# Who waits for a finished cell: ScalarE instead of GpSimd

## Chip, cores and metric

One NeuronCore of a Trainium2 chip runs the whole program. The time is that of the device for one execution, in microseconds (us); given is the median of several executions.

## What is computed

A graph block on 6250 nodes of 256 features and 200000 edges. With `xn` the normalised rows, three parts are added to `x`: a graph network of two layers, an attention without softmax, and after a second normalisation a router with two of eight experts.

```python
def _gnn_layer(x, row, col, W, b, g, beta):
    neigh = x[col]
    agg = jax.ops.segment_sum(neigh, row, num_segments=n)
    deg = jax.ops.segment_sum(jnp.ones((row.shape[0],), x.dtype), row, num_segments=n)
    deg = jnp.maximum(deg, 1.0)[:, None]
    h = (x + agg / deg) @ W.T + b
    ...
    return jax.nn.silu(hn)

x = x + _L0_gnn_ref(xn, edge_index, ...) + _L0_mix_ref(xn[None], ...)[0]
x = x + _L0_ffn_ref(_layernorm(x, axis=-1)[None], ...)[0]
```

The sum over neighbours is computed as a product with a dense matrix: `counts[source row, target column]` is how many edges lead from one node to the other. The change lies where this matrix is made.

## The kernel before

**The stages.** (1) To about 570 us: the edges' keys are sorted on VectorE with turns on TensorE, beside the attention's products. (2) From 571 to 1470 us: the count matrix is made, cell by cell. (3) To about 2000 us: the first graph layer, for which TensorE multiplies slabs of the count matrix with the table of rows (lines 1252, 1253). (4) The second layer (line 1255), and (5) from about 2600 us the experts.

**The count matrix.** It is cut in G = 637 cells: 13 row groups of 512 rows (`rg`), the last with 128 rows only, times 49 column blocks of 128. The sorted edges are cut in chunks of 128. A step is one chunk against one cell; there are STEPS = 2200 of them in a fixed walk through chunks and cells, and which step is the last of a cell depends on the edges. For a step, VectorE makes two one-hot tiles of the chunk's edges, 128 x 128 for the columns (`hot_c`, line 1946, eight steps at a time) and 128 x 512 for the rows (`hot_r`, line 1951), and TensorE multiplies them into the cell's bank of PSUM (line 1218). The steps are taken in groups of four; VectorE may be twelve `hot_r` tiles ahead.

**The banks.** Four banks take the cells in turn. When a cell's last step is done, ScalarE copies the bank, times 0.25, to `held` (line 866, semaphore `s_cell`) and clears it (line 867, `s_free`). After seven cells (`CW`) it stores them to the array `counts` in memory (line 870); the store waits for its last copy (`s_cell`), and the copy that reuses the half of `held` waits for the store of fourteen cells before (`s_held`, line 861). SyncE is the gate: for each group of four steps it loads from `cell1` which cell the group's last step belongs to, waits until `s_free` says that this cell's bank is clear, and increments `s_gate` (line 585); TensorE waits for `s_gate` and for VectorE's tiles (`s_hot`) before each group.

**Who knows that a cell is done.** TensorE increments `s_step` at each step. `ends` holds for each cell the number of steps after which it is complete; it is in SBUF, and becomes known only when the program runs. GpSimd walks through the cells: it loads `ends[g]` in a register (line 105, the helper `loaded`), waits until `s_step` has that value and increments `s_done` (line 696). ScalarE waits for `s_done >= g + 1`.

**What else is on GpSimd.** At cell 200 (`REST_AT`) it waits for the heavy cells (`s_heavy`) and writes their remainders to `rest` (line 693). Behind the loop it gathers the heavy rows of the table (`heavy_rows(0)`, line 706), when the table of 25 pairs has been written (line 542, `s_tab`), and then adds a bias to the rows of the first four pairs (`bias`, line 709), when `s_lo[0]` says that the table's low parts are made. Each further addition waits for a pair of the first layer. VectorE waits for the bias (`s_bias`) when it makes a pair's sums (`z_tile`, line 1983 and on).

Beside the steps run, in groups of fixed number, the output product of the attention (lines 1177, 1179), the table (lines 1910, 1911), the next pieces of the walk (lines 1083 to 1087, 1703), and from group 416 on the first 25-column halves of the first layer's sums (lines 1197, 1198).

Of the kernel before, what the change touches and what calls it, by code (L numbers as in the profile page):

```python
# [45 lines left out]
G = NRG * NCB  # L46
# [18 lines left out]
STEPS = -(-(NCH + G - 1) // 4) * 4  # L65
# [38 lines left out]
def loaded(nc, ap, engine, most):  # L104
    return nc.values_load_multi_w_load_instructions(
        ap, engines=(engine,), min_val=1, max_val=most,
        skip_runtime_bounds_check_because="one plus a cell's number, or a count of steps: both from the staircase")[1]
# [33 lines left out]
SLAB_AT = {**{AHEAD_AT - 4 + k: k for k in range(4)}, **{AHEAD_LAST[k] + 2: 4 + k for k in range(4)}}  # L141
assert len(SLAB_AT) == 8 and max(SLAB_AT) < STEPS // 4

REST_AT = 200

XF_BANKS = (0, 1, 3)
XF_LOWS = ((0, 2), (2, 3), (3, 5), (5, 7), (7, 9))
# [49 lines left out]
def gps_layer(nc, x, src, dst, w0, b0, g0, be0, w1, b1, g1, be1, wq, wkv, wo, bo,  # L197
              wr, br, fw1, fb1, fw2, fb2, ga, be, out):
    ctx = ExitStack()
    with ctx:  # L200
        def sb(name, shape, dt=F32):
            return ctx.enter_context(nc.sbuf_tensor(name, shape, dt))

        def sem(name):
            return ctx.enter_context(nc.semaphore(name))
# [9 lines left out]
        rest = nc.dram_tensor("remainders", [RB << 2 * CB_SH, 1], F16, kind="Internal").ap()  # L215
# [29 lines left out]
        hval = sb("heavy_value", [P, 2], F16)  # L245
# [40 lines left out]
        ends = outer[0:1, 10176:10496].bitcast(U16)  # L286
# [20 lines left out]
        h_cell, h_node, h_tmp, h_part = (heavy[:, n:n + 1].bitcast(I32) for n in (1, 2, 3, 4))  # L307
# [94 lines left out]
        s_heavy, s_hcell = sem("heavy_cells"), sem("heavy_cells_written")  # L402
# [3 lines left out]
        s_upto, s_uptop, s_ends = sem("cells_reached"), sem("cell_ends_product"), sem("cell_ends")  # L406
        s_hot, s_step, s_free = sem("one_hots"), sem("steps_done"), sem("cell_banks_free")

        s_gate, s_done = sem("groups_open"), sem("cells_done")
        s_cell, s_held = sem("cells_copied"), [sem("cells_stored0"), sem("cells_stored1")]  # L410
        s_xin, s_spill = [sem("x_pair_in0"), sem("x_pair_in1")], [sem("residual_out0"), sem("residual_out1")]
        s_dve = sem("dve_chain")
# [66 lines left out]
        def _(sp):  # L479
# [149 lines left out]
            with sp.Fori(1, NP - 1) as p:  # L629
                load_slabs(1, p)  # L630
            load_slabs(1, NP - 1, 1)

            sp.wait_ge(s_pick, 1)
            _, chosen = nc.values_load_multi_w_load_instructions(small[0:1, 64:66].bitcast(I32), engines=(mybir.EngineType.SP,),
                                                                 min_val=0, max_val=NE - 1)
            for k, v in enumerate(chosen):
# [18 lines left out]
        def _(pool):  # L655
# [30 lines left out]


            pool.wait_ge(s_zeroed, 16)
            pool.wait_ge(s_ends, 1)
            for g in range(G):  # L690
                if g == REST_AT:
                    pool.wait_ge(s_heavy, 1)
                    pool.indirect_dma_start(rest, bass.IndirectOffsetOnAxis(ap=h_cell, axis=0), hval[:, 0:1], None).then_inc(s_hcell, 16)
                end, = loaded(nc, ends[:, g:g + 1], mybir.EngineType.Pool, STEPS)
                pool.wait_ge(s_step, end)
                pool.sem_inc(s_done, 1)  # L696

            def affine(l, p):
                pool.wait_ge(s_nr[l], p + 1)
# [53 lines left out]
        def _(act):  # L753
# [100 lines left out]
            act.activation(hkeys, sort[home[ROUNDS]], ACT.Copy).then_inc(s_conv, 1)  # L854


            for g in range(G):
                b, c = g // CW % 2, g % CW
                act.wait_ge(s_done, g + 1)
                if c == 0 and g >= 2 * CW:  # L860
                    act.wait_ge(s_held[b], g // (2 * CW) * 16)
                rg, cb = g // NCB, g % NCB - c

                q = min(GR // P, RB - rg * (GR // P))
                cell_bank = bank[(g + 1) % NBK][:, 0:q * P]
                act.activation(held[:, b, 0:q, c, :], cell_bank.rearrange("p (q r) -> p q r", r=P), ACT.Copy, scale=0.25).then_inc(s_cell, 1)  # L866
                act.activation(cell_bank, cell_bank, ACT.Copy, scale=0.0).then_inc(s_free, 1)  # L867
                if c == CW - 1:
                    act.wait_ge(s_cell, g + 1)
                    act.dma_start(slabs[rg * GR:rg * GR + q * P, cb * P:(cb + CW) * P].rearrange("(q p) c -> p q c", p=P),  # L870
                                  held[:, b, 0:q, :, :].rearrange("p q c r -> p q (c r)")).then_inc(s_held[b], 16)
# [1418 lines left out]
```

## Time and profile before

| | us |
|---|---|
| median of 3 executions | 2919.98 (2918.04 to 2920.64) |
| the profiled execution | 2923.55 |
| its span, first to last instruction | 2921.8 |
| busy TensorE / VectorE / ScalarE / GpSimd | 2512.2 / 1878.7 / 1402.6 / 199.0 |

The profile is of one execution with the hardware profiler. PE is TensorE's matmul, PEld its weight load, DVE VectorE, ACT ScalarE, POOL GpSimd, SP SyncE; a q behind the name is the engine's queue, whose own work (register loads, waits, issues of DMAs) is not counted as busy. "L866 ... <- POOLq L696" is a wait of line 866 that GpSimd's line 696 ended. Instructions of an engine overlap at their ends, so the distance from start to start is shorter than the duration.

### The profile page before, as it was taken

The numbers are of one execution on the slowest core, as the hardware profiler recorded it, in microseconds if no ns is written. First come the engines' busy times: TensorE is split into PE (matmuls) and PEld (weight loads), VectorE is DVE, ScalarE is ACT, GpSimd is POOL, SyncE is SP. The second block draws the span as 40 slices with busy tenths as digits, with TensorE's granted clock in tenths as the row PEclk, the third lists the DMA queues.
The fourth block names the chain that finished last, engine by engine and source line by source line (L and its number), as shares of the span: only waits on it lengthen the run. The fifth ranks groups of instructions, "written<-read, shape, count | busy, mean of one in ns | idle before, by whom it ended". The sixth has DMA issues, their size and how long they took to land. (4 is left out here: it accounts for less than half of the span.)

```text
span 2921.8 us, 50327 instructions
## 1 busy us (share of the span) xinstructions
PE 2512.2 (86%) x14013; PEld 1458.1 (50%) x14013; DVE 1878.7 (64%) x4792; ACT 1402.6 (48%) x3753; POOL 199.0 (7%) x185
## 2 busy tenths in 40 slices
PE   0877677685889888889999999997999999969997
PEld 0444444332334343334378888883444444445665
DVE  8898887899999999999953222221333333366555
ACT  0877566265777667687821211211222222246665
POOL 0000000000000000000011111100111111115000
PEclk9998899698999999999999999998999999979999
DMA  5000000022245344243275555556444444410000
GB/s 182 19 15 15 11 15 15 17 76 76 89 146 185 116 162 161 103 165 136 102 256 185 157 162 165 157 162 208 140 135 140 141 135 141 140 33 15 22 22 31
DMA packets 167927, 318.02 MB, mean 109 GB/s; under 512 B 30227, under 2 KB 139540, under 8 KB 167764
## 3 DMA queue, kind: packets, MB, share of 16 engines
q1 hardware_dynamic: 115860, 230.55, 24.7%
q10 hardware_dynamic: 51776, 85.24, 8.0%
q8 instruction: 78, 1.28, 0.2%
q14 instruction: 85, 0.70, 0.1%
q0 software_dynamic: 128, 0.26, 0.1%
HBM read 203.09 MB, written 112.92 MB: 108 GB/s over the span
## 5 line engine op out<-in xcount | busy, mean ns | idle before, releaser
L1255 PE MATMUL banks<-outer,ring 128*128 128x512 f16 x2450 | 540.0, 380 | 18.6 <-DMA outer<-table,heavy 11.6
L866 ACT ACTIVATE ring<-banks 128x512 f16<-128x512 f32 (+1 forms) x637 | 365.6, 574 | 291.0 <-POOLq L696 287.9
L1252 PE MATMUL banks<-tabs,ring 128*128 128x257 f16 x2250 | 495.0, 274 | 3.3 <-DMA ring<-counts 3.3
L1253 PE MATMUL banks<-tabs,ring 128*128 128x256 f16 x2250 | 494.9, 273 | 0.0
L1255 PEld LDWEIGHTS banks<-outer,ring 128*128 128x128 f16 x2450 | 240.2, 98 | 299.8 <-issue 23.1
L867 ACT ACTIVATE banks<-banks 128x512 f32<-128x512 f32 (+1 forms) x637 | 367.0, 576 | 0.0
L1951 DVE TENSOR_SCALAR ring<-val,outer 128x512 f16<-128x512 f16 x1102 | 315.1, 345 | 20.0 <-PE banks L1218 19.9
L1218 PE MATMUL banks<-ring 128*128 128x512 f16 x920 | 261.4, 393 | 41.4 <-DVE ring L1951 20.1
L893 ACT ACT_TABLE_LOAD x50 | 64.2, 1283 | 377.7 <-DVE row_stats L2005 377.7
L1252 PEld LDWEIGHTS banks<-tabs,ring 128*128 128x128 f16 x2250 | 220.6, 98 | 31.8 <-issue 4.0
L1253 PEld LDWEIGHTS banks<-tabs,ring 128*128 128x128 f16 x2250 | 220.5, 98 | 25.8
L1024 PE MATMUL banks<-tabs,xT 128*128 128x512 f32 x400 | 203.3, 634 | 0.0
L1983 DVE TENSOR_SCALAR uinv<-banks 128x1 f32 (+1 forms) x49 | 7.7, 158 | 296.0 <-PE banks L1253 280.9
L1218 PEld LDWEIGHTS banks<-ring 128*128 128x128 f16 x920 | 85.6, 98 | 188.7 <-issue 133.9
L1951 DVE TENSOR_SCALAR outer<-val,outer 128x512 f16<-128x512 f16 x549 | 169.3, 345 | 7.5 <-PE banks L1218 7.1
L1408 PE MATMUL banks<-big,ring 128*128 128x256 f16 x1176 | 147.2, 275 | 20.8 <-DVE ring L2240 20.7
L1951 DVE TENSOR_SCALAR big<-val,outer 128x512 f16<-128x512 f16 x549 | 159.3, 345 | 0.0
L1395 PE MATMUL banks<-outer,big 128*128 (+2 forms) x624 | 147.8, 373 | 4.2 <-DVE big L2184 4.2
L2240 DVE SCALAR_TENSOR_TENSOR ring<-ring,product_scales 128x512 f16<-128x512 f32 (+1 forms) x104 | 83.0, 808 | 100.7 <-ACT ring L980 100.5
L1218 PE MATMUL banks<-outer,ring 128*128 128x512 f16 x276 | 94.0, 390 | 60.4 <-DVE big L1951 45.3
L1408 PEld LDWEIGHTS banks<-big,ring 128*128 128x128 f16 x1176 | 113.7, 98 | 59.9 <-DVE ring L2240 27.7
L2002 DVE BATCH_NORM_STATS2 row_stats<-xn 128x6 f32 (+1 forms) x100 | 37.4, 416 | 152.2 <-ACT xn L887 152.2
(391 smaller groups left out, 3816.7 us busy)
## 6 DMA issues: line engine op xcount, KB each, us to landing
counts<-ring ACTq DMA_DIRECT2D x84, 896.0 KB, 4.1
ring<-counts SPq DMA_DIRECT2D x94, 800.0 KB, 4.7
ring<-counts SPq DMA_DIRECT2D x94, 768.0 KB, 4.1
outer<-in_fw SPq DMA_DIRECT2D x8, 1024.0 KB, 8.2
outer<-in_x SPq DMA_DIRECT2D x5, 1280.0 KB, 13.5
x_transposed<-xT SPq DMA_DIRECT2D x50, 128.0 KB, 1.7
outer<-in_x SPq DMA_DIRECT2D x25, 256.0 KB, 3.0
xT<-x_transposed SPq DMA_DIRECT2D x25, 256.0 KB, 2.8
```

The costliest lines, as they stand in the source:

```text
L866: act.activation(held[:, b, 0:q, c, :], cell_bank.rearrange("p (q r) -> p q r", r=P), ACT.Copy, scale=0.25).then_inc(s_cell, 1)
L867: act.activation(cell_bank, cell_bank, ACT.Copy, scale=0.0).then_inc(s_free, 1)
L893: act.activation(std_of(n, b), var_of(n, b), ACT.Sqrt, bias=eps_c[:, :]).then_inc(s_std[n], 1)
L1024: m = mm(bank[4 + h], xT[t % 2][:, c * P:(c + 1) * P], wkv_s[:, c * 1024 + h * 512:c * 1024 + (h + 1) * 512], start=c == 0, stop=c == DC - 1)
L1218: mm(ps[:, bass.ds(at, 512)], hot_c[t // 8 % 3][:, t % 8, :], hot_r[t % RSLOTS], start=False, stop=False, skip_group_check=True).then_inc( ...
L1252: mm(o[:, 0:D + 1], a, xtab[l][:, COLUMN[cb], D:2 * D + 1], start=cb == 0, stop=False)
L1253: m = mm(o[:, 0:D], a, xtab[l][:, COLUMN[cb], 0:D], start=False, stop=cb == NT - 1)
L1255: m = mm(o, a, xtab[l][:, COLUMN[cb], 0:2 * D], start=cb == 0, stop=cb == NT - 1)
L1395: m = mm(bank[4 + j % 4][:, 0:nt * P], w1p[:, a, w:w + P], xfp[:, bass.ds(g * 4, nt), b * D + c * P:b * D + (c + 1) * P], start=c == a == ...
L1408: m = mm(bank[q][:, 0:D], hp[:, j % 4, a, q * P:(q + 1) * P], w2p[:, b, j * D:(j + 1) * D], start=j == a == b == 0, stop=j == FJ - 1 and a ...
L1951: ins = dve.tensor_scalar(hot_r[t % RSLOTS], iota16[:, 0:GR], row_v[:, q % 2, u:u + 1], None, op0=ALU.is_equal)
L2240: dve.scalar_tensor_tensor(hp[:, j % 4, 1, 0:w], hid[j % 2][:, 0:w], fsc[:, 2:3], hp[:, j % 4, 0, 0:w], op0=ALU.mult, op1=ALU.subtract).th ...
```

## The change

ScalarE loads `ends[g]` in a register of its own, once for each cell, and waits for `s_step` itself. GpSimd's loop of 637 loads, waits and increments, and the semaphore `s_done`, are gone. The write of the remainders no longer stands at cell 200 of that loop but alone, behind its wait for the heavy cells; what stood behind the loop on GpSimd follows it directly.

```diff
--- before.py
+++ after.py
@@ -141,7 +141,6 @@
 SLAB_AT = {**{AHEAD_AT - 4 + k: k for k in range(4)}, **{AHEAD_LAST[k] + 2: 4 + k for k in range(4)}}
 assert len(SLAB_AT) == 8 and max(SLAB_AT) < STEPS // 4
 
-REST_AT = 200
 
 XF_BANKS = (0, 1, 3)
 XF_LOWS = ((0, 2), (2, 3), (3, 5), (5, 7), (7, 9))
@@ -406,7 +405,7 @@
         s_upto, s_uptop, s_ends = sem("cells_reached"), sem("cell_ends_product"), sem("cell_ends")
         s_hot, s_step, s_free = sem("one_hots"), sem("steps_done"), sem("cell_banks_free")
 
-        s_gate, s_done = sem("groups_open"), sem("cells_done")
+        s_gate = sem("groups_open")
         s_cell, s_held = sem("cells_copied"), [sem("cells_stored0"), sem("cells_stored1")]
         s_xin, s_spill = [sem("x_pair_in0"), sem("x_pair_in1")], [sem("residual_out0"), sem("residual_out1")]
         s_dve = sem("dve_chain")
@@ -686,14 +685,8 @@
 
 
             pool.wait_ge(s_zeroed, 16)
-            pool.wait_ge(s_ends, 1)
-            for g in range(G):
-                if g == REST_AT:
-                    pool.wait_ge(s_heavy, 1)
-                    pool.indirect_dma_start(rest, bass.IndirectOffsetOnAxis(ap=h_cell, axis=0), hval[:, 0:1], None).then_inc(s_hcell, 16)
-                end, = loaded(nc, ends[:, g:g + 1], mybir.EngineType.Pool, STEPS)
-                pool.wait_ge(s_step, end)
-                pool.sem_inc(s_done, 1)
+            pool.wait_ge(s_heavy, 1)
+            pool.indirect_dma_start(rest, bass.IndirectOffsetOnAxis(ap=h_cell, axis=0), hval[:, 0:1], None).then_inc(s_hcell, 16)
 
             def affine(l, p):
                 pool.wait_ge(s_nr[l], p + 1)
@@ -854,9 +847,11 @@
             act.activation(hkeys, sort[home[ROUNDS]], ACT.Copy).then_inc(s_conv, 1)
 
 
+            act.wait_ge(s_ends, 1)
             for g in range(G):
                 b, c = g // CW % 2, g % CW
-                act.wait_ge(s_done, g + 1)
+                end, = loaded(nc, ends[:, g:g + 1], mybir.EngineType.Activation, STEPS)
+                act.wait_ge(s_step, end)
                 if c == 0 and g >= 2 * CW:
                     act.wait_ge(s_held[b], g // (2 * CW) * 16)
                 rg, cb = g // NCB, g % NCB - c
```

ScalarE's instructions around a store, before. `cells_done` is `s_done`, `cells_copied` is `s_cell`, `cells_stored0` is one of `s_held`:

```order
L866 ACTIVATE ring<-banks 128x4x128 [waits cells_done]
L867 ACTIVATE banks<-banks 128x512
L870 DMA counts<-ring 128x4x896 [waits cells_copied]
L866 ACTIVATE ring<-banks 128x4x128 [waits cells_stored0,cells_done]
L867 ACTIVATE banks<-banks 128x512
```

The same place with the change (its lines 861, 862 and 865 are 866, 867 and 870 of before); `steps_done` is `s_step`:

```order
L861 ACTIVATE ring<-banks 128x4x128 [waits steps_done]
L862 ACTIVATE banks<-banks 128x512
L865 DMA counts<-ring 128x4x896 [waits cells_copied]
L105 TENSOR_LOAD outer
L861 ACTIVATE ring<-banks 128x4x128 [waits cells_stored0,steps_done]
L862 ACTIVATE banks<-banks 128x512
L105 TENSOR_LOAD outer
```

A load stands in front of each copy, and behind the store's issue where there is one; the copy waits for the steps where it waited for GpSimd.

GpSimd between the last fill of stage 1 and the first loop of the first layer, before:

```order
L685 MEMSET tabs 128x2048 [waits dots_added]
L105 TENSOR_LOAD outer [waits cell_ends,remainders_cleared]
L105 TENSOR_LOAD outer [waits steps_done] x199
L693 DMA remainders<-heavy_value,heavy 802816x1 [waits steps_done,heavy_cells]
L105 TENSOR_LOAD outer
L105 TENSOR_LOAD outer [waits steps_done] x436
L706 DMA tabs<-table,heavy 128x512 [waits steps_done,table0_written]
L709 TENSOR_TENSOR xn<-xn,big 128x512 [waits table0_low]
L709 TENSOR_TENSOR xn<-xn,big 128x512 x3
```

and with the change (its lines 689, 699 and 702 are 693, 706 and 709 of before):

```order
L684 MEMSET tabs 128x2048 [waits dots_added]
L689 DMA remainders<-heavy_value,heavy 802816x1 [waits heavy_cells,remainders_cleared]
L699 DMA tabs<-table,heavy 128x512 [waits table0_written]
L702 TENSOR_TENSOR xn<-xn,big 128x512 [waits table0_low]
L702 TENSOR_TENSOR xn<-xn,big 128x512 x3
```

None of the three waits for `steps_done` any more, only for its own data.

## Rows read from the trace of the kernel before

**Rows 1.** Busy us (instructions) by stretch: PE, PEld, DVE, ACT, POOL; clock, DMA, GB/s
```profile
606.00:1441.00 835.00, 712.78 (x2982) 294.75 (x2979) 812.03 (x2560) 599.39 (x1158) 1.19 (x1) 0.96 0.37 130
1441.00:1470.00 29.00, 22.66 (x107) 9.29 (x107) 25.34 (x81) 19.45 (x92) 0.00 (x0) 1.00 0.18 69
```

**Rows 2.** Groups by line, 571 to 1471 us: busy us, mean ns, idle before
```profile
L1951 DVE TENSOR_SCALAR ring<-val,outer 128x512 f16<-128x512 f16 x1101 | 314.8, 345 | 20.0 <-PE banks L1218 19.9
```

**Rows 3.** Waits, 606 to 1441 us: us in total, times, longest
```profile
ACT ring L866 <- POOLq L696: 237.0, 186, 23.2
...
PE banks L1218 <- SPq L585: 32.2, 49, 1.7
...
DVE ring L1951 <- PE banks L1218: 16.4, 25, 3.5
```

**Rows 4.** The same, 1441 to 1470 us
```profile
PE banks L1218 <- SPq L585: 6.8, 14, 0.8
DVE ring L1951 <- PE banks L1218: 2.5, 5, 0.7
```

**Rows 5.** Instructions of lines 105 and 870: duration in ns, min/median/max
```profile
L105 POOLq TENSOR_LOAD <-outer x637: 268/274/1333, 570.1 to 1469.4; - x160
L870 ACTq DMA_DIRECT2D counts<-ring x91: 338/378/451, 592.7 to 1470.1; - x91
```

**Rows 6.** Order of time from 1280 us: start and duration in us
```profile
1280.27 0.70 PE L1218 MATMUL banks<-outer,ring 128*128 128x512 f16 x2
...
1281.06 0.60 ACT L866 ACTIVATE ring<-banks 128x512 f16<-128x512 f32 x1 [0.23 <-POOLq L696]
```

**Rows 7.** Order of time from 300 us
```profile
300.71 1.91 PE L1031 MATMUL banks<-big,xT 128*128 128x256 f32 x4
...
302.66 0.38 ACT L768 ACTIVATE xn<-banks 128x256 f32<-128x256 f32 x1 [1.41 <-PE banks L1031]
```

**Rows 8.** Order of time on ScalarE from 1301 us
```profile
1302.47 0.61 ACT L866 ACTIVATE ring<-banks 128x512 f16<-128x512 f32 x1
...
1303.46 0.61 ACT L866 ACTIVATE ring<-banks 128x512 f16<-128x512 f32 x1
1303.94 0.62 ACT L867 ACTIVATE banks<-banks 128x512 f32<-128x512 f32 x1
1304.11 0.38 ACTq L870 DMA_DIRECT2D counts<-ring  x1
1304.76 0.60 ACT L866 ACTIVATE ring<-banks 128x512 f16<-128x512 f32 x1 [0.20 <-POOLq L696]
```

**Rows 9.** ScalarE at 2094 us: order of time, and line 878 alone
```profile
2094.00 1.28 ACT L893 ACT_TABLE_LOAD   x1 [2.30 <-DVE row_stats L2005]
L878 ACTq ALU_OP  x1: 35/35/35, 2094.1 to 2094.1; - x1
```

**Rows 10.** Lines 542 and 709, and busy time in two stretches
```profile
L542 SPq DMA_DIRECT2D table<-tabs x25: 359/367/463, 830.9 to 1267.8; - x25
L709 POOL TENSOR_TENSOR xn<-xn,big x25: 1252/1265/1276, 1471.6 to 1917.3; 128x512 f32 x21, 128x512 f32<-128x512 f32 x4
1270.00:1277.00 7.00, 5.60 (x21) 1.91 (x20) 7.00 (x25) 5.15 (x11) 0.00 (x0) 1.00 0.70 234
1281.00:1441.00 160.00, 150.42 (x779) 67.58 (x779) 159.44 (x532) 138.48 (x272) 0.00 (x0) 1.00 0.39 139
```

**Rows 11.** Line 2240 in two stretches of equal length, and line 749
```profile
2635.00:2671.00 36.00, 19.84 (x14) 1.00 0.00 1
2671.00:2707.00 36.00, 9.56 (x13) 1.00 0.09 30
L749 POOL TENSOR_TENSOR xn<-xn,xT x25: 1258/1710/1722, 2635.1 to 2670.4; 128x512 f32 x25
```

**Rows 12.** Order of time at 1477 us, and a wait from 1466 to 1500
```profile
1477.59 0.38 PE L1252 MATMUL banks<-tabs,ring 128*128 128x257 f16 x1 [2.70 <-DMA ring<-counts]
DVE uinv L1983 <- PE banks L1315: 15.1, 1, 15.1
```

## The prediction

> **What bounds the kernel now.** I read the views in this order: busy time by stretch, groups by line, waits, and then the order of time at single places. The change touches one stretch, from 571 to 1470 us, in which 637 cells of the count matrix are made. In its body, 606 to 1441 us, VectorE is busy for 812.0 of 835 us, 97%, TensorE for 712.8 and ScalarE for 599.4 [rows 1]. VectorE's share is the one-hot tiles of line 1951 [rows 2]: it is the pacer, and a microsecond taken from ScalarE is worth nothing there by itself. The last 49 cells are another matter: from 1441 to 1470 us VectorE is busy 25.3 of 29 us, TensorE 22.7, ScalarE 19.5, so no engine is full and the loop from step to copy to gate sets the pace [rows 1].
>
> The waits say how much hangs on the part that changes. In the body ScalarE sits idle for 237.0 us in front of line 866 until GpSimd signals a cell, but that is mostly ScalarE having nothing to do: the signal comes when the step has been done. What counts is who waits for ScalarE: TensorE waits for SyncE's gate 49 times, 32.2 us together, and VectorE, the pacer, waits for TensorE in front of the largest group of line 1951 for 16.4 us [rows 3]. In the last 29 us TensorE waits for the gate 14 times, 6.8 us together, about half a microsecond in each group of four steps, and VectorE 2.5 us [rows 4]. That is the room that a faster signal could win.
>
> **The signal.** Removed are 637 loads, 637 waits and 637 increments on GpSimd. Their time there was free; what they cost is the hop. At 1280.97 us (1280.27 + 0.70) the matmul that ends a cell is over, and ScalarE starts at 1281.06: 0.09 us [rows 6]. Where ScalarE waits for TensorE itself, the matmul of 302.62 us (300.71 + 1.91) is followed at 302.66: 0.04 us [rows 7]. So 0.05 us is saved for each cell for which ScalarE stands waiting. Of these, only a signal in front of a gate that TensorE stands at, and whose delay VectorE then feels, shortens the run: the 14 gates of the end [rows 4], and I take about 7 of the 49 in the body, since VectorE is full through most of them. 21 x 0.05 = 1.0 us gained. The bound below is that every gate counts, 63 x 0.05 = 3.2 us.
>
> **The load on ScalarE.** Added are 637 loads in ScalarE's queue. On GpSimd one takes 0.274 us, the longest 1.33 [rows 5]. ScalarE works off cells that are ready at one per 0.99 us (1302.47 to 1303.46) [rows 8]. Is the load beside that or added to it? Two rows say beside. The store of line 870 is issued at 1304.11 while the clearing of line 867 runs until 1304.56 [rows 8]. And at 2094.1 the queue does a register operation of line 878, which stands behind an activation, while the table load in front of that activation has just begun, at 2094.00, and has 1.28 us to go [rows 9]. So the queue runs ahead of the engine; 0.27 us hides under the copy and the clearing of the cell before, and even a load of 0.9 us would. I cost it at nothing inside a block of seven. If the cover goes, the price is in the first rival.
>
> The exception is the seventh cell. Its store waits in the queue for the copy, takes 0.38 us to issue [rows 5], and only behind it can the next load start. The issue ended at 1304.49 [rows 8], and the load adds its 0.27 us and the steps around it, together some 0.32 us, to the earliest start of the next copy. There are 90 such places. Most have slack, as here, where the next cell was ready only at 1304.76. I take it that six are in front of a gate that matters, four of the seven in the last stretch, where cells come at the pace of the loop, and two in the body: 6 x 0.32 = 1.9 us lost. The bounds are 0 and, if 30 places counted, 9.6 us. The Trainium skill gives a `tensor_load` a floor of about 600 ns (DMA: Bandwidth & Descriptors, Latency and other measured facts); by it the six places would cost 2 us more, as an estimate; the trace has 0.274 us, and the sum goes by that.
>
> **What GpSimd does with its freedom.** Behind its loop stand three things that now come early. The write of the remainders moves from behind cell 200 to the moment the heavy cells are known; nobody waits for it until the slabs are read. The gather of the heavy rows moves from behind the last cell to shortly after the last write of the table, issued at 1267.8 [rows 10]. And the first four bias additions of line 709, 1.265 us each, follow it [rows 10]. Before, they began at 1471.6 us, while VectorE waited 15.1 us for TensorE [rows 10, 12]. Now they fall in about 1270 to 1277 us, where it is busy for 7.00 of 7.00 us [rows 10]. What they would do beside line 1951 no row shows. The nearest rows: from 2635 to 2671 us GpSimd adds (line 749) while VectorE runs line 2240, 14 instructions in 19.84 us, 1.42 each; in the next 36 us, without GpSimd, 13 take 9.56, 0.74 each; and GpSimd's own addition is stretched from 1.26 to 1.71 us [rows 11]. In the 1.71 us of one addition VectorE thus does 1.71 x 0.74 / 1.42 = 0.89 us of work and loses 0.82. Four additions: 3.3 us. The end below is 0 (line 1951 has one tile input, where 2240 has two), a gain is excluded, since nothing that VectorE waits for in the stage comes from GpSimd; the end above is the whole of the additions, 4 x 1.265 = 5.1 us. I take 3.3, from the only contended pair of the trace. VectorE is full for 159.4 of the 160 us behind it, so it is carried to the end of the stretch [rows 10].
>
> Having these early buys nothing: the next stretch begins with TensorE waiting for slabs, until 1477.59 us, and the first use of sums by VectorE waits for TensorE's line 1315, not for the bias [rows 12]. The stretch behind is bound by TensorE and is only shifted.
>
> **The sum.** -1.0 + 1.9 + 3.3 = +4.2 us. The profiled execution took 2923.55 us (span 2921.8), 3.6 above the median of the runs, 2919.98. The terms are differences, so I put them on the median: 2924.2, rounded to 2924.0.
>
> **Rivals.**
> - *The load does not hide* (7%). If the queue takes the load only when the clearing has ended, a ready cell costs 0.48 to the clearing, 0.62 for it, 0.27 for the load: at least 1.37 us instead of 0.99. 588 large cells x 1.37 = 806 us, the 49 small ones some 35, and 84 stores x 0.38 = 32: 873 of 899 us, and since cells come in bursts it would be the bound for much of the time; I price it at +40 us, 2960. It decides from the point where ScalarE's time per cell passes 1.4 us, the stretch's 899 / 637. Against it stand [rows 8, 9].
> - *GpSimd takes VectorE's inputs for the whole of each addition* (18%): VectorE stands still for 5.1 us, and ten store places count instead of six: -1.0 + 3.2 + 5.1 = +7.3, 2927.3. For it: 1951 is full just there [rows 10]. Against: in [rows 11] both engines slow down, neither stops. The Trainium skill says this outright: the loser of the shared port "fully blocks" (SBUF — State Buffer, Who interferes with whom); these rows don't bear the word "fully" out.
> - *The additions cost nothing* (25%), because VectorE's tiles come first and GpSimd works in between: +0.9, or with three store places 0: 2920 to 2921. For it: one tile input.
> - *The hop counts more* (12%). The long loads, up to 1.33 us [rows 5], now and then made GpSimd late; a queue that runs ahead takes them out. If each of the 63 gates gives 0.05 (3.2 us), the late signals at the end another 4, and the additions cost nothing, the time is 2913.
>
> The rest, 38%, is my forecast.
>
> **How the numbers follow.** 0.2% of the time, 5.8 us, is about what a measurement of this kernel can tell from no change. The forecast (+4.2) and the third rival (+0 to +1) lie within it, with a part of the forecast's own spread beyond: same 0.55. Slower: rivals one and two, 0.25, and 0.07 of the forecast: 0.32. Faster: most of the last rival, and a little of the third: 0.13. The range leaves out the first rival and the outer half of the last one: 2914 to 2931, the upper end being full blocking (+5.1) with some 20 store places (+6.4) less the hop.
>
> **What would show it.** Right: in the changed profile line 105 stands in ScalarE's queue 637 times at about 0.27 us; copies in a burst still start 0.99 us apart; a copy starts 0.04 us behind its matmul; behind a store the next copy starts 0.3 us later than before; the additions of the bias stand near 1272 us with VectorE's instructions beside them at over 0.35 us, and the last cell is copied at about 1474 us, not just before 1470. Wrong: a pitch of 1.3 us or more (the first rival), tiles of line 1951 that keep their 0.345 us through the additions [rows 2] (the third), or a stretch between 1441 and 1470 us that is shortened by more than 1 us (the last).

## The result, and the profile after

The changed kernel takes 2926.78 us in the median of 15 executions (2920.74 to 2930.55), the kernel before 2918.67 us (2915.99 to 2923.71) beside it on the same chip. The two medians lie 8.1 us apart. The ratio estimated from all executions is 1.0023, with a 95% interval of 1.0015 to 1.0031: slower by 0.23%, some 4 to 9 us, 6.7 by its middle. The range, 2914 to 2931, holds the time. The predicted 2924.0 is 2.8 too low, but that flatters it: the kernel before was 1.3 us faster here than in the three executions that the forecast started from. As a difference, +4.2 was forecast and +6.7 to +8.1 measured.

The spans of the two profiled executions, 2921.8 and 2923.7 us, show 1.9 us of that, because the first stage happened to end 5 us earlier in the later one. So all comparisons of traces below start at the first step and count from there. The largest group of the steps' matmuls in the changed kernel, which holds the first and the last of the 2200 (how many, duration in ns, start of the first and of the last):

```profile
L1213 PE MATMUL banks<-ring x920: 379/380/634, 566.9 to 1472.1; 128*128 128x512 f16 x184
```

Before, the same row says 572.0 to 1469.3. The 2200 steps thus take 905.2 us instead of 897.3: **7.9 us longer**.

(Lines shift a little: 1951, 866 and 870 of before are 1946, 861 and 865 in the changed kernel; in the experiments 1951 is 1946 to 1951.)

Busy time by stretch, as in [rows 1], the second stretch up to 1473 us since the last cell is later:

```profile
606.00:1441.00 835.00, 707.34 (x2954) 292.58 (x2952) 811.29 (x2543) 593.13 (x1146) 8.87 (x6) 0.96 0.37 128
1441.00:1473.00 32.00, 23.80 (x113) 9.65 (x113) 26.98 (x85) 20.53 (x99) 0.00 (x0) 1.00 0.20 72
```

VectorE is still the pacer, 811.3 of 835 us. TensorE has 5.4 us less to its name than before: fewer steps were done in the same time. Waits in the body, and from 1441 us on, to compare with [rows 3, 4]:

```profile
ACT ring L861 <- PE banks L1213: 238.7, 194, 23.1
...
PE banks L1213 <- SPq L584: 29.4, 46, 2.1
...
DVE ring L1946 <- PE banks L1213: 13.8, 25, 1.3
```

```profile
PE banks L1213 <- SPq L584: 8.0, 13, 1.1
DVE ring L1946 <- PE banks L1213: 3.7, 7, 0.8
```

ScalarE now waits for TensorE itself, 238.7 us against 237.0 for GpSimd's signal. TensorE's wait for the gate is 29.4 us instead of 32.2, and VectorE's for TensorE 13.8 instead of 16.4. In the tail it goes the other way: 8.0 us for the gate instead of 6.8, and 3.7 instead of 2.5. Neither is 7.9 us. Most of it stands in one place, in the order of time on VectorE (start, duration; a row holds up to six neighbours of a kind):

```profile
1265.65 0.68 DVE L1941 TENSOR_TENSOR ring<-outer 128x1024 f16<-128x1024 f16 x1
1266.26 0.34 DVE L1946 TENSOR_SCALAR outer<-val,outer 128x512 f16<-128x512 f16 x1
1266.52 6.03 DVE L1946 TENSOR_SCALAR big<-val,outer 128x512 f16<-128x512 f16 x3
1272.47 0.87 DVE L1946 TENSOR_SCALAR ring<-val,outer 128x512 f16<-128x512 f16 x3
```

The third row is three tiles that take 6.03 us; three of them take 0.87 elsewhere. The second of the three, from 1266.78 us, alone has 5.50 us. Beside it, GpSimd:

```profile
1264.48 2.71 POOL L699 DMA_INDIRECT tabs<-table,heavy  x1 [581.95 <-DMA table<-tabs]
1267.21 4.91 POOL L702 TENSOR_TENSOR xn<-xn,big 128x512 f32<-128x512 f32 x4
```

And busy time of each engine just before, in and behind the stretch (columns as in [rows 1]):

```profile
1260.00:1267.20 7.20, 5.06 (x19) 1.72 (x18) 7.20 (x23) 5.08 (x10) 2.71 (x1) 1.00 0.20 73
1267.20:1272.20 5.00, 0.09 (x1) 0.00 (x0) 5.00 (x1) 1.09 (x2) 4.91 (x4) 0.89 1.04 317
1272.20:1277.00 4.80, 4.12 (x10) 1.52 (x11) 4.80 (x17) 2.00 (x4) 0.00 (x0) 0.50 0.49 182
```

The four additions, 4.91 us, and VectorE's stop lie on one another. VectorE counts as busy for 5.00 of 5.00 us but finishes nothing; TensorE does 0.09 us of work, and as it starts again its granted clock is 0.50, the lower level of 1.2 GHz, in the stretch behind. The gather of line 699 takes 2.71 us here.

Step by step, the 7.9 us come together like this: 0.55 less up to step 1600, 5.46 more between steps 1600 and 1700, 1.5 more between 1800 and 1900, 0.2 more from there to 2130, and 1.35 more in the tail. The 1.5 goes with a drop of TensorE's granted clock to 0.50 at 1335.9 us. Such a drop is in eight of the twelve profiled executions of this document, and not in those of the kernel before and of experiments 2, 6 and 9. Whether the change makes it more frequent, no run shows.

ScalarE around a store, to be held against [rows 8]:

```profile
1302.24 0.61 ACT L861 ACTIVATE ring<-banks 128x512 f16<-128x512 f32 x1
...
1303.23 0.62 ACT L861 ACTIVATE ring<-banks 128x512 f16<-128x512 f32 x1
...
1303.88 0.38 ACTq L865 DMA_DIRECT2D counts<-ring  x1
1304.66 0.60 ACT L861 ACTIVATE ring<-banks 128x512 f16<-128x512 f32 x1 [0.32 <-PE banks L1213]
```

Copies that are ready start 0.99 us apart (1302.24 to 1303.23), as before. Behind the store the next copy starts 0.40 us after the issue has ended (1303.88 + 0.38 to 1304.66). That is its floor now: in 44 of the 90 places the distance is 0.39 to 0.41 us, and nowhere less. Before, it was 0.10 us in 35 of them, as here in the tail (1443.39 + 0.35 to 1443.84):

```profile
1443.39 0.35 ACTq L870 DMA_DIRECT2D counts<-ring  x1
1443.84 0.28 ACT L866 ACTIVATE ring<-banks 128x128 f16<-128x128 f32 x1 [0.31 <-issue]
```

And the loads themselves:

```profile
L105 ACTq TENSOR_LOAD <-outer x637: 257/263/1349, 565.0 to 1472.1; - x160
```

### The profile page after: what moved, and what is told of

It is laid out like the page before. It is cut to its first block and busy times, and to the rows that moved or that the text cites. A ratio compares the mean times of both kernels' runs of the same rounds, so it can differ in the third digit from the quotient of the medians.

```text
span 2923.7 us, 49690 instructions
## 1 busy us (share of the span) xinstructions
PE 2507.3 (86%) x14013; PEld 1456.0 (50%) x14013; DVE 1882.3 (64%) x4792; ACT 1400.1 (48%) x3753; POOL 200.7 (7%) x185
## 5 line engine op out<-in xcount | busy, mean ns | idle before, releaser
L1019 PE MATMUL banks<-tabs,xT 128*128 128x512 f32 x400 | 196.5, 615 | 0.0
L1403 PEld LDWEIGHTS banks<-big,ring 128*128 128x128 f16 x1176 | 114.0, 98 | 61.1 <-DVE ring L2235 28.6
L694 POOL TENSOR_TENSOR xn<-xn,big 128x512 f32 (+1 forms) x49 | 62.0, 1266 | 1155.0 <-DVE xn L2009 1115.9
```

The source lines that it names most:

```text
L1019: m = mm(bank[4 + h], xT[t % 2][:, c * P:(c + 1) * P], wkv_s[:, c * 1024 + h * 512:c * 1024 + (h + 1) * 512], start=c == 0, stop=c == DC - 1)
L1403: m = mm(bank[q][:, 0:D], hp[:, j % 4, a, q * P:(q + 1) * P], w2p[:, b, j * D:(j + 1) * D], start=j == a == b == 0, stop=j == FJ - 1 and a ...
```

## The experiments

Kernels were run in three sets, the kernel before beside each: its median was 2919.61 us in the first set (27 executions), 2920.84 in the second (33) and 2920.74 in the third (15). "Steps" is the time from the first to the last of the 2200 steps in the profiled execution, less that of before, cut at step 2130, where the small cells begin. One such number can be off by 1.5 us: where the drop of TensorE's clock near 1335 us occurs, the steps begin 1.2 to 1.5 us later from there on, and before's profile doesn't have it. A ratio from 10 or 11 executions has an interval of 0.09% to either side, 2.6 us.

### 1. The additions put back behind the last cell (first set)

```diff
@@ on GpSimd, ahead of the gather
+            pool.wait_ge(s_step, STEPS)
             heavy_rows(0)
```

> The change, but GpSimd waits for all 2200 steps before it gathers the heavy rows and adds the bias, so that both stand where they stood before the change. Theory A (GpSimd's four additions stop VectorE altogether): the instruction of 5.5 us on line 1946 is gone and no tile takes over 0.4 us; 5.2 us of the 8.1 come back, the median is some 2.5 us above the kernel before. Rival B (the load behind each store is the main cost, and the additions only stand beside VectorE): at most 1 us comes back, the median stays some 7 us above before.

Measured: 2919.44 us (11 executions), ratio 1.0005 (0.9996 to 1.0014). The long tile is gone. Steps: -0.28 us up to 2130, +1.72 in the tail. So ScalarE's loads and waits by themselves cost 1.5 us by the ratio, within the noise, where 2.5 us were expected. The new place of what stands behind the loop costs the difference between 1.0023 and 1.0005, 5.3 us, which can be off by 3.5; the trace has 5.46 us for it. This experiment moves gather and additions together; the next one parts them.

### 2. The gather early, the additions late (first set)

```diff
@@ on GpSimd
             heavy_rows(0)
+            pool.wait_ge(s_step, STEPS)
             pool.wait_ge(s_lo[0], NP)
```

> The change, but GpSimd waits for all steps between the gather of the heavy rows and the bias additions: the gather is early, the additions late. Theory A: the gather costs VectorE nothing although it takes 2.7 us itself, so the time is that of e1_late within 1 us. Rival B (a gather beside VectorE takes its port as well): 1 to 2.7 us above e1_late, with a tile of line 1946 of over 1 us near 1265 us.

Measured: 2919.52 us, 1.0002 (0.9993 to 1.0011). GpSimd, and VectorE's tiles beside the gather:

```profile
1265.06 3.96 POOL L699 DMA_INDIRECT tabs<-table,heavy  x1 [581.37 <-DMA table<-tabs]
1465.97 4.94 POOL L702 TENSOR_TENSOR xn<-xn,big 128x512 f32<-128x512 f32 x4 [196.95 <-PE banks L1214]
```

```profile
1266.98 0.87 DVE L1947 TENSOR_SCALAR big<-val,outer 128x512 f16<-128x512 f16 x3
```

The gather takes 3.96 us instead of the 0.97 that it took alone behind the last cell, but three of VectorE's tiles beside it take their 0.87 us. It is GpSimd's work that takes longer here. Steps 1600 to 1660 take what they took before, within 0.03 us. The cost is the additions' alone.

### 3. Eight additions early instead of four (first set)

```diff
-            for p in range(4):
+            for p in range(8):
                 bias(p)
```

with the loop behind it shortened by four.

> The change, with eight bias additions ahead of the loop where there are four, so that eight of them run in a row near 1267 us. Theory A (VectorE stands still for as long as GpSimd adds): one tile of line 1946 of about 10.4 us, and the time 5 us above the change's 2926.8, some 13 us above before. Rival B (my estimate of 0.82 us lost per addition, the rest from elsewhere): 3.3 us above the change. Rival C (the four additions are not what costs): no difference.

Measured: 2930.48 us (5 executions), 1.0039 (1.0025 to 1.0053). VectorE and GpSimd:

```profile
1268.47 10.89 DVE L1946 TENSOR_SCALAR big<-val,outer 128x512 f16<-128x512 f16 x3
```

```profile
1269.16 9.79 POOL L702 TENSOR_TENSOR xn<-xn,big 128x512 f32<-128x512 f32 x8
```

9.79 us of additions, and one tile of 10.37 us in the group of three. Twice the additions, twice the stop. Four more cost 0.16% more, 4.7 us, for 4.9 us of work. The ratios alone are too coarse to tell that from rival B's 3.3 us, and the time is 11 us above before, not 13. The traces do tell: the steps lose 10.14 us here and 5.46 with four, 4.7 us for four more. The stop is the whole of each addition, not a share of it.

### 4. The load ahead of the store (first set)

Experiment 1, and the next cell's load is issued behind the clearing, so that the store comes after it:

```diff
+            end, = loaded(nc, ends[:, 0:1], mybir.EngineType.Activation, STEPS)
             for g in range(G):
-                end, = loaded(nc, ends[:, g:g + 1], mybir.EngineType.Activation, STEPS)
                 act.wait_ge(s_step, end)
...
                 act.activation(cell_bank, cell_bank, ACT.Copy, scale=0.0).then_inc(s_free, 1)
+                if g + 1 < G:
+                    end, = loaded(nc, ends[:, g + 1:g + 2], mybir.EngineType.Activation, STEPS)
                 if c == CW - 1:
```

> As e1_late, and ScalarE loads the next cell's last step behind the clearing of the cell before it, ahead of the store's issue, so that no load stands behind a store. Theory A (the load behind the store costs 0.32 us where a gate waits for it): the first copy behind a store starts 1.1 us after the last one ahead of it, as before the change, not 1.4; the end of the stage, 1441 to 1470 us, is 1.3 to 2 us shorter than in e1_late, and the median falls 2 to 3 us below e1_late, to 0 to 1 us below before. Rival B (loads are hidden behind stores too): the same time as e1_late.

Measured: 2919.05 us, 0.9998 (0.9989 to 1.0007). Around a store:

```profile
1306.10 0.38 ACTq L868 DMA_DIRECT2D counts<-ring  x1
1306.58 0.60 ACT L862 ACTIVATE ring<-banks 128x512 f16<-128x512 f32 x1
```

The next copy follows the end of the issue by 0.10 us (1306.10 + 0.38 to 1306.58), as in the tail before the change. Steps: +0.24 us up to 2130, -0.42 in the tail, where experiment 1 had +1.72 and the other kernels with the load behind the store +1.3 to +1.8. The load behind a store thus costs 1.8 to 2.1 us, all of it in the seven places of the tail: 7 x 0.29 = 2.0. The median can't show it: 0.9998 and 1.0005 are 2.0 us apart, with intervals that overlap. Up to step 1600, experiments 1 and 4 lie at -1.7 and -1.2: the stores of the body cost nothing that shows.

### 5. Two loads for each cell, the first try (second set)

```diff
+                loaded(nc, ends[:, g:g + 1], mybir.EngineType.Activation, STEPS)
                 end, = loaded(nc, ends[:, g:g + 1], mybir.EngineType.Activation, STEPS)
```

> As e1_late, but ScalarE loads each cell's last step twice. Theory A (a load hides under the copy and the clearing, and shows only behind a store and between the small cells of the end): cells that are ready still follow each other at 0.99 to 1.01 us in the body; the first copy behind a store starts another 0.3 us later; from step 2130 to step 2199 the steps take 2 to 5 us longer than in e1_late (the small cells' pitch of 0.4 us can't hold two loads); the median is 2 to 6 us above e1_late. Rival B (loads add to each cell): a pitch of 1.27 us for ready cells and a median over 20 us above e1_late. Rival C (nothing of the load shows anywhere): the same time.

Measured: 2919.91 us, 0.9996 (0.9987 to 1.0005). But the trace has only 637 loads in ScalarE's queue: the compiler left out the one that nothing used. It is experiment 1 once more, and says nothing on its question; experiment 9 asks it again. It has a use as a measure of the noise: what is the same program came out at 1.0005 in the first set and at 0.9996 here.

### 6. Fills in place of the additions (second set)

The gather early and the additions late, as in experiment 2; in the additions' early place GpSimd fills three tiles of the same size that nobody needs then, so this is work added to the program:

```diff
+            for free in (g_s, xT[0][:, :], xT[1][:, :]):
+                pool.memset(free, 0.0)
+            pool.wait_ge(s_step, STEPS)
```

> As e2_gather_early (gather early, bias late), and GpSimd fills three tiles of 128x512 that nobody needs any more where the change has its additions, near 1268 us; they only write. Theory A (any instruction of GpSimd on SBUF stops line 1951, a read or not): one tile of it lasts as long as the three fills together, some 1.5 us more, and the time is 1.5 us above e2_gather_early. Rival B (it is the reads of the additions that stop VectorE): all tiles at 0.35 us, no difference.

Measured: 2922.0 us (10 executions), 1.0004 (0.9995 to 1.0013). VectorE and GpSimd:

```profile
1264.44 2.81 DVE L1949 TENSOR_SCALAR big<-val,outer 128x512 f16<-128x512 f16 x3
```

```profile
1265.11 0.54 POOL L706 MEMSET big<- 128x512 f32 x1
1265.57 1.00 POOL L706 MEMSET xT<- 128x512 f32 x2
```

The three tiles of VectorE take 2.81 us instead of 0.87, with 1.54 us of fills beside them, and steps 1600 to 1660 take 1.9 us longer. One of the three tiles alone has 2.29 us. That is read from the trace; the median, 1.0004 against 1.0002 in experiment 2, is too coarse to show 1.5 us. A fill reads nothing from SBUF, and it stops VectorE too. So it is not GpSimd's reading that collides.

### 7. The four additions spaced out (second set)

One each behind steps 1680, 1760, 1840 and 1920:

```diff
             for p in range(4):
+                pool.wait_ge(s_step, 1680 + 80 * p)
                 bias(p)
```

> The change, but GpSimd's four additions stand singly, behind steps 1680, 1760, 1840 and 1920, not in a row. Theory A (VectorE is the pacer, each addition takes it for 1.25 us wherever it stands in the body): four tiles of line 1946 of some 1.5 us, and the same time as the change, 7 to 8 us above before. Rival B (a stop of 1.25 us is absorbed by the twelve tiles that VectorE is ahead, only one of 5 us in a row reaches TensorE, and it is the fall of TensorE's clock behind the long stop that costs): 3 us or less above before.

Measured: 2924.95 us, 1.0016 (1.0007 to 1.0025). Steps 1600 to 2000: +5.6 us, of which some 1.3 is the clock's drop near 1335 us, by the other traces that have it. The first of the four, on VectorE and on GpSimd:

```profile
1285.94 0.68 DVE L1942 TENSOR_TENSOR ring<-outer 128x1024 f16<-128x1024 f16 x1
1286.54 1.35 DVE L1947 TENSOR_SCALAR outer<-val,outer 128x512 f16<-128x512 f16 x1
```

```profile
1285.04 2.71 POOL L702 TENSOR_TENSOR xn<-xn,big 128x512 f32<-128x512 f32 x1 [12.41 <-PE banks L1214]
```

A tile of 1.35 us instead of 0.34, four times. Both sizes were missed: the run is 4.7 us above before by its ratio (2 to 7), not 7 to 8 and not 3 or less. For rival B's reason nothing speaks: single stops do reach the steps, each by about 1 us. Spacing gains at most a little. Four lone tiles lose 1.0 us each against 5.2 for the one of the change, and the ratios, 1.0016 and 1.0023, overlap.

GpSimd's row is 2.71 us long, though an addition takes 1.26: it stands from 1285.04, through VectorE's tiles of line 1947. If its last 1.26 us are the work, they begin at 1286.49, close to the end of line 1942 (1286.62), which compares two inputs. The same holds, to 0.01 us, for all four here and for three of the four in experiment 8; the last one there began between two tiles of line 1947. So while VectorE goes from one such tile to the next GpSimd is mostly shut out, it comes in at the end of the other kind, and then shuts VectorE out.

### 8. The four additions in the tail (second set)

As 7, behind steps 2144, 2152, 2160 and 2168.

> The change, but the four additions stand behind steps 2144, 2152, 2160 and 2168, in the stretch of the small cells, where VectorE is not the pacer. Theory A (a stop costs where VectorE is full, and is free where the gate sets the pace): long tiles are there, but the time is that of e1_late within 1.5 us. Rival B (a stop costs wherever it falls): 4 to 5 us above e1_late.

Measured: 2921.27 us, 0.9999 (0.999 to 1.0008). The first addition on GpSimd:

```profile
1443.14 1.65 POOL L702 TENSOR_TENSOR xn<-xn,big 128x512 f32<-128x512 f32 x1 [172.90 <-PE banks L1214]
```

There are again four tiles of about 1.35 us, between 1443.6 and 1455.2 us, so VectorE is stopped as in 7. Yet the tail is 1.3 us longer than before and experiment 1's is 1.7 longer, experiment 2's 1.3: the stop costs nothing. VectorE has slack in the tail, as [rows 1, 4] say, and none in the body. The price of a stop is set by where it falls.

### 9. Two loads for each cell, both used (third set)

Experiment 1, with a load of the cell before and a wait on it as well:

```diff
+                if g:
+                    prev, = loaded(nc, ends[:, g - 1:g], mybir.EngineType.Activation, STEPS)
                 end, = loaded(nc, ends[:, g:g + 1], mybir.EngineType.Activation, STEPS)
+                if g:
+                    act.wait_ge(s_step, prev)
                 act.wait_ge(s_step, end)
```

> As e1_late (additions behind the last cell), with a second load per cell in ScalarE's queue, of the previous cell's last step, which a second wait uses, so that it stays in the program: 1273 loads. Theory A (the queue works ahead beside copy and clearing; only behind a store is the load in the open): inside a block ready copies still start 0.99 to 1.01 us apart, behind a store the next copy starts another 0.25 to 0.35 us later (store end to copy about 0.7 instead of 0.39), and the run is 1 to 5 us longer than e1_late: 1.0015 of before, about 2923. Rival (a load takes its time from the engine): ready copies start at least 0.25 us further apart, 1.25 or more, and the run is over 10 us longer.

Measured: 2968.15 us (5 executions), 1.0157 (1.0143 to 1.017): 46 us slower. Both theories missed. Away from the stores, ready large cells keep their pitch of 0.99 us, as theory A says, but the time is far past its 1 to 5 us. ScalarE behind a store in the body, and the loads of that stretch:

```profile
1303.99 0.38 ACTq L870 DMA_DIRECT2D counts<-ring  x1
1305.94 0.60 ACT L866 ACTIVATE ring<-banks 128x512 f16<-128x512 f32 x1 [1.50 <-PE banks L1218]
...
1307.44 0.60 ACT L866 ACTIVATE ring<-banks 128x512 f16<-128x512 f32 x1 [0.41 <-issue]
```

```profile
L105 ACTq TENSOR_LOAD <-outer x6: 262/366/865, 1304.4 to 1307.8; - x6
```

Loads issued while the store's data moves (it lands 4.1 us after its issue, in the median) are slow: here there are two of 0.85 and 0.87 among the six. In experiment 1, 87 of its 637 loads take over 0.7 us, the longest 1.37, and all of them start 0.8 to 3.4 us behind a store's issue. It is not ScalarE's queue that makes them slow: GpSimd's loads of before show the same behind stores, with 0.8 us in the mean 1 to 2 us after the issue. One load of 0.8 us hides under a large cell of 0.99 us; a slow one and a second one do not. Here the next copy starts 1.57 us behind the end of the issue (1303.99 + 0.38 to 1305.94), and the one after it another 1.50 us later. This place is worse than most for the first copy: its floor is 0.77 to 0.79 us behind a store, where experiment 1 has 0.39, which is what theory A expected. What theory A lacked is the second copy: it follows the first within 1.02 us behind 42 of 84 stores of large cells in experiment 1, and behind 4 here, where most take 1.6 to 2.0 us. The waits in the body:

```profile
PE banks L1218 <- SPq L584: 65.6, 75, 2.7
...
DVE ring L1951 <- PE banks L1218: 33.5, 46, 2.3
```

TensorE's wait for the gate is 65.6 us against 28.6 in experiment 1, VectorE's for TensorE 33.5 against 15.2. In the tail, first this kernel, then experiment 1:

```profile
1496.85 0.28 ACT L866 ACTIVATE ring<-banks 128x128 f16<-128x128 f32 x1 [0.75 <-PE banks L1218]
...
1497.55 0.28 ACT L866 ACTIVATE ring<-banks 128x128 f16<-128x128 f32 x1 [0.25 <-PE banks L1218]
...
1498.25 0.28 ACT L866 ACTIVATE ring<-banks 128x128 f16<-128x128 f32 x1 [0.25 <-issue]
```

```profile
1454.79 0.28 ACT L862 ACTIVATE ring<-banks 128x128 f16<-128x128 f32 x1 [0.69 <-PE banks L1214]
...
1455.16 0.27 ACT L862 ACTIVATE ring<-banks 128x128 f16<-128x128 f32 x1
...
1455.51 0.28 ACT L862 ACTIVATE ring<-banks 128x128 f16<-128x128 f32 x1
```

A small cell needs 0.70 us instead of 0.35 to 0.37: there the queue, not the engine, sets the pitch, and the second load and wait add 0.33 to 0.35 to each cell. Steps: +32.7 us up to 2130, +12.8 behind it. The cover under which one load hides is thus about one load deep.

### 10. The load ahead of the store and the gather early (third set)

Experiments 4 and 2 together.

> The load placed ahead of the store (as e4_ahead) and the gather of the heavy rows early, the additions behind the last cell (as e2_gather_early). Theory A: no tile of line 1946 or 1949 over 1 us near 1267 us, the tail from step 2130 to 2199 no longer than before, the run 2918 to 2920, within 0.1% of before. Rival (the early gather costs something that single profiles hid): 2 us or more above e4_ahead.

Measured: 2916.06 us (11 executions), 0.9986 (0.9977 to 0.9995), below the 2918 to 2920 expected. It is the one version that comes out ahead of the kernel before, by 0.14%, less than the 0.2% that such a comparison can be trusted with, and so ahead of the change by 0.37%. Its steps are 0.2 us longer than before's in the profiles, so the trace doesn't show where the 4 us lie, and the interval meets that of experiment 4; 0.12% between the two is little more than the 0.09% between experiments 1 and 5, the same program. That it is no slower than before is shown; that the early gather adds to it isn't.

## Why the prediction was right or wrong

The sum said +4.2 us: the signal -1.0, the load behind the store +1.9, the additions +3.3.

**The signal** is as forecast where it can be read directly. Of the copies that wait for their cell's last step, 212 of 220 start 0.09 us behind the matmul before, and 211 of 221 start 0.04 us behind it in experiment 4, with the load ahead of the store. In the changed kernel 189 of 244 do; the rest come up to 0.4 us later, because the load is late. What the signal is worth in the body is less certain. Up to step 1600, where nothing else has changed, the steps come 0.55 us earlier in the changed kernel, and between 0.6 and 1.9 earlier in experiments 1 to 8 and 10. But experiments 1 and 5, the same program, stand at 1.7 and 0.6. In the small cells there is a gain that the step didn't have: with GpSimd's walk their usual pitch was 0.40 us, with ScalarE's own it is 0.35 to 0.37. With the load out of the way of the store the tail is 0.4 us shorter than before (experiment 4). The forecast had 0.7 for the tail.

**The load hidden inside a block** held: the pitch of ready cells is 0.99 us. The reason given, that "even a load of 0.9 us would" hide, was needed: over 80 loads take 0.7 us or more, a few up to 1.35. What it lacked is how thin this cover is. The first rival's +40 us is about what the second load costs (experiment 9, +46), though not by its mechanism: away from the stores the pitch of ready large cells didn't move; it is behind stores and in small cells that the queue falls behind.

**The load behind the store** held in sum, 1.9 against 1.8 to 2.1, not in its places. All seven of the tail count, not four, and none in the body that shows, not two. The price of one was forecast at 0.32 and is 0.29 us. That the sum came out is luck in part: two wrong counts made up for each other.

**The additions** are the step that failed: +3.3 predicted, 5.3 measured by experiment 1 and 5.46 in the trace (steps 1600 to 1700 of the changed kernel against before). The step is "In the 1.71 us of one addition VectorE thus does 1.71 x 0.74 / 1.42 = 0.89 us of work and loses 0.82": VectorE does none of it then. The row was near enough; it was read wrongly. [Rows 11] give means over a stretch, 1.42 us instead of 0.74 for line 2240 and 1.71 instead of 1.26 for the addition, and they look like two engines that slow each other down. The single instructions say something else. GpSimd's, and then VectorE's, before the change:

```profile
2641.37 1.27 POOL L749 TENSOR_TENSOR xn<-xn,xT 128x512 f32 x1
2642.59 1.72 POOL L749 TENSOR_TENSOR xn<-xn,xT 128x512 f32 x1
2644.27 1.26 POOL L749 TENSOR_TENSOR xn<-xn,xT 128x512 f32 x1
2645.49 1.72 POOL L749 TENSOR_TENSOR xn<-xn,xT 128x512 f32 x1
```

```profile
2641.60 1.58 DVE L2240 SCALAR_TENSOR_TENSOR ring<-ring,product_scales 128x512 f16<-128x512 f32 x1 [1.32 <-ACT ring L980]
2644.24 1.84 DVE L2240 SCALAR_TENSOR_TENSOR ring<-ring,product_scales 128x512 f16<-128x512 f32 x1 [1.06 <-ACT ring L980]
2646.86 0.90 DVE L2240 SCALAR_TENSOR_TENSOR ring<-ring,product_scales 128x512 f16<-128x512 f32 x1 [0.78 <-ACT ring L980]
```

Each of the 14 instructions of line 2240 in that stretch ends 0.55 us behind the end of the addition that was running when it began, whether it took 0.90 or 1.84 us in all (2641.37 + 1.27 = 2642.64, and 2641.60 + 1.58 = 2643.18). And the additions have two lengths, 1.26 us and 1.72: 14 of the 25 are of the long kind, one for each instruction of VectorE, which they waited for. The two take turns, and each holds the other off for a whole instruction, but for some 0.2 to 0.3 us at the ends (an instruction of line 2240 alone takes 0.74 us). The mean of 1.42 came from VectorE arriving in the middle of additions, and from its having only 14 instructions to do there; it said nothing of the loss of a VectorE that is always busy. That loss is the whole addition. One thing is different beside line 1946, and why stays open: an instruction of line 2240 gets its turn after one addition, while a tile of line 1946 waits through all four, or all eight, in a row. That line 1946 has one tile input, which the prediction took as a reason for less, was none.

The second rival, full blocking at 18%, had the mechanism, and 2927.3 against 2926.78. The closeness of the time is luck in part: it counted ten store places for 3.2 us, where about 2 is measured, it started from a median of before 1.3 us higher than the one beside the change, and it has no term for the clock's drop near 1335 us. Its further mark, that VectorE stands still for 5.1 us, is the tile of 5.50 us, behind which the next one starts 5.2 us late.

The Trainium skill (SBUF — State Buffer, Who interferes with whom) says it in this way: an instruction with two inputs meets only those GpSimd instructions that read SBUF, a VectorE instruction in a two-port mode meets all of them, and whichever comes first keeps the ports for the whole instruction while the other is fully blocked. The traces agree on the full blocking, for line 1946 (experiments 3 and 7) and, by the rows above, for line 2240. Fills, which only write, stop a tile of line 1946 too (experiment 6), so that line behaves like the two-port kind; its mode is in no trace, and fills beside line 2240 were not tried. The prediction quoted the rule and set it aside with the words that the rows don't bear "fully" out. They did.

**What carried the chances.** Same at 0.55 was the likeliest, slower by over 0.2% had 0.32, and the result is 0.23% with an interval on both sides of that bound. With the additions at their full 5.1, the sum would have been +6.0 and the odds the other way round. The gather, which the prediction moved along at no cost, did cost nothing, though it took 2.7 to 4.1 us instead of 0.97. And **having these early buys nothing** held as far as the ratios can tell: experiment 1 has them late and is the faster by 0.18%.

## What to carry to other kernels

When a wait or a loop is taken off an engine, what stood behind it runs early; ask beside which instructions of the other engines it now falls, and if it is not needed early, pin it where they have slack. Read the price of a collision from single instructions, start and end of both, and not from means over a stretch: a mean of twice the usual length looked like sharing and was a whole wait, met at its middle. A register load in a queue is free as long as it is in the shadow of the instruction before; put it ahead of a slow issue such as a store, and count how many loads the shadow holds before adding a second.

## What the runs showed of the hardware

- VectorE's 128x512 f16 tiles with one tile input (0.27 us from start to start) and GpSimd's additions or fills exclude each other: 5.50 us for one tile beside four additions, 10.37 beside eight, 1.35 beside one. A tile that waits is recorded as busy. It works both ways: a lone addition of 1.26 us was on record with 2.71, and in seven of eight cases its last 1.26 us began as VectorE ended a two-input instruction (experiments 7 and 8).
- A two-input instruction (line 2240) and GpSimd's additions exclude each other as well, but in turns: VectorE's ended 0.55 us behind the addition in progress 14 times out of 14, and the addition behind it took 1.72 us instead of 1.26.
- A gather that GpSimd issues took 0.97 us with VectorE idle and 2.7 to 4.1 us beside such tiles, and did not slow them (3.96 us in experiment 2, tiles at 0.34).
- A register load from SBUF in ScalarE's queue takes 0.26 us, but 0.8 in the mean between 1 and 2 us behind the issue of a store, while its data moves, and 1.37 at the longest (experiment 1). The Trainium skill's floor of about 600 ns for a `tensor_load` (DMA: Bandwidth & Descriptors, Latency and other measured facts) doesn't hold here: the 637 loads have a median of 0.263 us, and the measurement decides. ScalarE's queue runs such a load beside the copy ahead of it: in experiment 1 one of 0.52 us from 1306.42 stands beside a copy from 1306.38 to 1306.98.
- After 5 us in which TensorE did nothing, its granted clock was 0.50 in the 4.8 us behind. VectorE lost 5.16 us at that tile and the steps lost 5.46, so it cost 0.3 us at most. The same drop near 1335 us, where TensorE is busy for 150.4 of 160 us [rows 10], cost 1.2 to 1.5 us.
